# Scale rows gathered ahead, weights unpacked in the feed-forward, and the rotary sum on VectorE

## The reference

```python
q = _apply_rope(q, curr_seq_pos)
k = _apply_rope(k, curr_seq_pos)
raw = jnp.einsum('bhqd,bhkd->bhqk', q, k) / scale
attn = jax.nn.softmax(raw + mask, axis=-1)
...
w = (qw[:, None, :] >> shifts[None, :, None] & MAXQ).reshape(-1, qweight.shape[1])
s = scales[g_idx]
return (w.astype(scales.dtype) - z[g_idx].astype(scales.dtype)) * s
...
h = jax.nn.silu(xf @ Wg) * (xf @ Wu)
out = h @ Wd
```

## Time and profile before

| | |
|---|---|
| Median of 3 runs | 1169.86 us (1169.71 to 1169.95) |
| The profiled execution, its own time | 1171.48 us |
| Its span, first to last instruction | 1169.7 us |
| PE busy | 1037.1 us, 89% |
| DVE busy | 796.0 us, 68% |
| POOL busy | 457.7 us, 39% |
| ACT busy | 349.8 us, 30% |
| Mean granted TensorE clock | 0.946 of 2.4 GHz |

### The profile page before, as it was taken

How to read it: one execution, slowest core, us unless ns; L and a number is a source line. 1 busy time by engine, 2 the same in 40 slices (tenths; PEclk the granted TensorE clock), 3 DMA queues, 4 the chain that set the end, 5 groups by cost and what they waited for, 6 DMA issues and landing times. The chain is left out here.

```text
span 1169.7 us, 13349 instructions
## 1 busy us (share of the span) xinstructions
PE 1037.1 (89%) x4696; PEld 741.4 (63%) x4696; DVE 796.0 (68%) x1251; ACT 349.8 (30%) x926; POOL 457.7 (39%) x296
## 2 busy tenths in 40 slices
PE   5688877877878799999999999999999986999998
PEld 2333333344557567777777677677777765888787
DVE  4899998759566687778878888787676655222223
ACT  3232332213212332333333333333343332222131
POOL 3566655445515443444434434434243102222121
PEclk8899998869888899999999999999999998999999
DMA  7000000000311332332333325421010005211001
GB/s 258 1 1 0 1 1 1 1 18 1 104 50 52 118 123 78 127 112 88 109 100 118 126 80 168 161 97 45 27 46 18 1 2 168 53 38 32 1 1 72
DMA packets 60962, 75.91 MB, mean 65 GB/s; under 512 B 8444, under 2 KB 44068, under 8 KB 60888
## 3 DMA queue, kind: packets, MB, share of 16 engines
q1 hardware_dynamic: 56032, 57.66, 15.7%
q0 software_dynamic: 4144, 17.04, 4.5%
q10 hardware_dynamic: 720, 0.36, 0.1%
HBM read 64.37 MB, written 10.68 MB: 64 GB/s over the span
## 5 line engine op out<-in xcount | busy, mean ns | idle before, releaser
L1301 POOL TENSOR_TENSOR shared<-shared 128x512 f32<-128x512 f32 x64 | 83.7, 1307 | 201.6 <-DVE shared L1435 201.3
L754 PE MATMUL ps<-woh,oh 128*128 128x512 f32 x256 | 108.8, 425 | 32.9 <-DVE ol L1465 28.1
L1370 ACT ACTIVATE c_xn<-c_xn,c_mn 128x64 f32<-128x64 f32 x256 | 86.0, 337 | 155.6 <-DVE c_mn L1449 155.6
L754 PE MATMUL ps<-xh,wqh 128*128 128x512 f32 x256 | 106.6, 416 | 0.4 <-DVE shared L1435 0.4
L756 PE MATMUL ps<-woh,ol 128*128 128x512 f32 x256 | 104.7, 409 | 0.0
L755 PE MATMUL ps<-wol,oh 128*128 128x512 f32 x256 | 104.3, 408 | 0.0
L1433 DVE TENSOR_TENSOR shared<-ps,cs 128x512 f32<-128x512 f32 x80 | 54.9, 687 | 70.6 <-PE ps L756 70.6
L756 PE MATMUL ps<-xh,wql 128*128 128x512 f32 x256 | 100.4, 392 | 0.0
L755 PE MATMUL ps<-xl,wqh 128*128 128x512 f32 x256 | 99.9, 390 | 0.0
L540 DVE TENSOR_TENSOR r<-ps,vpad 128x512 f32<-128x512 f32 x128 | 79.4, 683 | 27.4 <-PE ps L629 27.4
L372 POOL TENSOR_TENSOR r<-r 128x1024 f32<-128x1024 f32 x32 | 77.1, 2410 | 50.4 <-DVE r L540 50.3
(11 more groups left out here) (172 smaller groups left out, 2387.8 us busy)
## 6 DMA issues: line engine op xcount, KB each, us to landing
stage<-in_wq SPq DMA_DIRECT2D x16, 512.0 KB, 4.1
stage<-in_wo SPq DMA_DIRECT2D x16, 512.0 KB, 3.8
w_wide<-dq SPq DMA_DIRECT2D x32, 172.0 KB, 4.9
wf<-w_wide SPq DMA_DIRECT2D x20, 256.0 KB, 3.4
qraw<-in_gate_qweight SPq DMA_DIRECT2D x16, 172.0 KB, 4.3
qraw<-in_up_qweight SPq DMA_DIRECT2D x16, 172.0 KB, 3.7
qraw<-in_down_qweight SPq DMA_DIRECT2D x10, 256.0 KB, 4.5
w_down<-dq SPq DMA_DIRECT2D x10, 256.0 KB, 6.0
```

The source lines that it names most:

```text
L754: pe.matmul(dst, lh, rh, start=(first and c == 0), stop=False)
L1301: pool.tensor_tensor(qT[:, h * TPH:(h + 1) * TPH, :, p - 1, :], turn(ra), turn(rb), ALU.add)\
L1370: act.activation(part, part, ACT.Exp, scale=-1.0, bias=mn[:, c % 2, u:u + 1], accum_out=sm[:, c % 2, u:u + 1]).then_inc(exp_ready, 1)
```

## The change

1. **Rotary sum.** `rotary_sum` is moved word for word from POOL's list to DVE's: behind `add` for the first rotary product of a step, right behind `rotary` for the second.
2. **Gate and up.** The attention steps no longer make these weights. POOL gathers their scale and zero rows, SP stores them as they are to a new HBM tensor `sz_wide`, and `gate_up` loads for each tile the packed integers (four loads of 64 KB, each row repeated eight times) and the rows of zeros and scales (two loads of 256 KB), and DVE unpacks, subtracts and multiplies there, into `wf`. Three buffers are used in turn.
3. **Down.** Its 11 units are made in the attention as before, but spread: `fetch_plan` gives every step number with n mod 4 = 2 a down unit and the others a gate/up unit, for n = 2 to 44. POOL issues the gather of step n's unit in step n-1, and waits first until the unit two before it in the plan is through (`fetch_done`): for a gate/up unit until its rows are stored, for a down unit until DVE has multiplied.
4. `wd` is loaded behind tile 5 instead of tile 3.

```diff
+def fetch_plan():
+    plan, wide, down, n = {}, 0, 0, 2
+    while wide < WIDE_UNITS or down < NTI:
+        if n % TPH == DOWN_AT and down < NTI:
+            plan[n] = (len(plan), WIDE_UNITS + down)
+            down += 1
+        elif n % TPH != DOWN_AT and wide < WIDE_UNITS:
+            plan[n] = (len(plan), wide)
+            wide += 1
+        n += 1
+    return plan
...
+def fetch_done(eng, g, f):
+    u = next(unit for number, unit in PLAN.values() if number == f)
     if u < WIDE_UNITS:
+        same = [v for number, v in PLAN.values() if number <= f and number % 2 == f % 2 and v < WIDE_UNITS]
+        eng.wait_ge(g["sz_stored"][f % 2], 16 * len(same))
     else:
+        eng.wait_ge(g["wd_ready"], u - WIDE_UNITS + 1)
...
+def fetch_scales(pool, g, f, u):
+    if f >= 2:
+        fetch_done(pool, g, f - 2)
+    table = g["table_wide"] if u < WIDE_UNITS else g["table_down"]
+    pool.indirect_dma_start(g["sz"][:, f % 2, 0:width_of(u)], None, table,
...
+def store_scales(sp, g, f, u):
+    chunk, q = u // QPIECES, u % QPIECES
+    sp.wait_ge(g["sz_landed"][f % 2], 16 * (f // 2 + 1))
+    sp.dma_start(g["sz_wide"][chunk * P:(chunk + 1) * P, :, q * QCOLS:(q + 1) * QCOLS],
...
 # rotary_attention, SP, step
                     load_number(PIECES * (2 * (b + db) + odd) + piece + 2)
-                u = unit_at(n)
-                if u is not None:
-                    if 2 <= u + 2 < Q_UNITS:
-                        load_packed(sp, a, g, u + 2)
-                    store_weights(sp, g, u)
+                if n - 1 in PLAN:
+                    f, u = PLAN[n - 1]
+                    if u < WIDE_UNITS:
+                        store_scales(sp, g, f, u)
+                    else:
+                        store_down(sp, g, u - WIDE_UNITS)
+                if n in PLAN and WIDE_UNITS <= PLAN[n][1] < Q_UNITS - 2:
+                    load_down(sp, a, g, PLAN[n][1] - WIDE_UNITS + 2)
...
 # rotary_attention, POOL, step
-                if projecting(c, last):
-                    for p in ROTARY_OF[j]:
-                        rotary_sum(b, sl + 1, p)
                 due = piece_due(c, last)
                 if due:
                     piece, db, odd = due
                     low_piece(pool, g, b + db, odd, piece)
-                u = unit_at(step_number(b, c))
-                if u is not None and u + 2 < Q_UNITS:
-                    gather_scales(pool, g, u + 2)
+                ahead = step_number(b, c) + 1
+                if ahead in PLAN:
+                    fetch_scales(pool, g, *PLAN[ahead])
...
 # rotary_attention, DVE, step
-                u = unit_at(step_number(b, c))
-                if u is not None:
-                    subtract_zeros(dve, g, u)
+                f, u = PLAN.get(step_number(b, c), (0, 0))
+                t = u - WIDE_UNITS
+                if t >= 0:
+                    subtract_zeros(dve, g, f, t)
                 units = ROTARY_OF[j] if projecting(c, last) else ()
                 for p in units[:1]:
                     rotary(b, sl + 1, p)
                 if tile_exists(c - 3, last):
                     add(b, c - 3, last)
+                for p in units[:1]:
+                    rotary_sum(b, sl + 1, p)
                 if early and tile_exists(c - 2, last):
                     low_out(b, c - 2)
                 if tile_exists(c, last):
                     probabilities(b, c)
-                if u is not None:
-                    multiply_scales(dve, g, u)
+                if t >= 0:
+                    multiply_scales(dve, g, f, t)
                 for p in units[1:]:
                     rotary(b, sl + 1, p)
-                if u is not None and u + 1 < Q_UNITS:
-                    unpack_weights(dve, g, u + 1)
+                    rotary_sum(b, sl + 1, p)
+                if 0 <= t < NTI - 1:
+                    unpack_down(dve, g, t + 1)
...
 # gate_up, SP
+                if k >= 3:
+                    sp.wait_ge(w_ready, k - 2)
+                for c in range(DC):
+                    src = bass.AP(q.tensor, q.offset + packed * c * INTER + P * t, [[INTER, packed], [0, PACK], [1, w]])
+                    sp.dma_start(raw[:, k % 3, c * P:c * P + w], src).then_inc(landed[k % 3], 16)
+                rows = g["sz_wide"][m * DC * P:(m + 1) * DC * P, :, t * P:t * P + w].rearrange("(c p) e n -> p e c n", p=P)
+                for e in range(2):
+                    sp.dma_start(columns(sz[:, k % 3, e, :], k), rows[:, e, :, :]).then_inc(landed[k % 3], 16)
+                if k == 5:
...
 # gate_up, DVE
+            for i in range(2, NT):
+                norm_rows(dve, g, n, xn, i)
+                norm_low(dve, g, n, XT, i - 2)
+                if i in DEQUANT_AT:
+                    dequantise(DEQUANT_AT[i])
+            norm_low(dve, g, n, XT, NT - 2)
+            norm_low(dve, g, n, XT, NT - 1)
+            dequantise(2)
+            dequantise(3)
             for t in range(NTI):
                 w = inner(t)
+                if t + 2 < NTI:
+                    unpack(2 * t + 4)
+                    subtract(2 * t + 4)
+                    unpack(2 * t + 5)
+                    scale(2 * t + 4)
+                    subtract(2 * t + 5)
+                    scale(2 * t + 5)
```

More of the change, by code:

```diff
@@ L853, in gather_scales @@
[L853 to L867, removed]
@@ L870, in subtract_zeros @@
[L870 to L886, removed]
@@ L889, in store_weights @@
[L889 to L899, removed]
+DOWN_AT = 2
+def fetch_plan():
[9 more added lines that the diff above has]
+    return plan
@@ new lines, in load_down, with unpack_down @@
+def load_down(sp, a, g, t):
+    rows = inner(t)
+    if t >= 2:
+        sp.wait_ge(g["q_used"], t - 1)
+    w = a["down_qweight"]
+    src = bass.AP(w.tensor, w.offset + P // PACK * t * D, [[D, rows // PACK], [0, PACK], [1, D]])
+    sp.dma_start(g["qraw"][0:rows, t % 2, :], src).then_inc(g["q_landed"][t % 2], 16)
+def unpack_down(dve, g, t):
+    raw = g["qraw"][0:inner(t), t % 2, :]
+    dve.wait_ge(g["q_landed"][t % 2], 16 * (t // 2 + 1))
+    dve.tensor_scalar(raw, raw, g["nib"][0:inner(t), 0:1], 15, ALU.logical_shift_right, ALU.bitwise_and).then_inc(g["qn_ready"], 1)
@@ new lines, in subtract_zeros, with multiply_scales @@
+def subtract_zeros(dve, g, f, t):
+    w = inner(t)
+    dve.wait_ge(g["qn_ready"], t + 1)
+    dve.wait_ge(g["sz_landed"][f % 2], 16 * (f // 2 + 1))
+    if t >= 2:
+        dve.wait_ge(g["w_stored"][t % 2], 16 * (t // 2))
+    dve.tensor_tensor(g["dq"][0:w, t % 2, :], g["qraw"][0:w, t % 2, :], g["sz"][0:w, f % 2, D:2 * D], ALU.subtract)\
+       .then_inc(g["q_used"], 1)
+def multiply_scales(dve, g, f, t):
+    w = g["dq"][0:inner(t), t % 2, :]
+    dve.wait_ge(g["q_used"], t + 1)
+    dve.tensor_tensor(w, w, g["sz"][0:inner(t), f % 2, 0:D], ALU.mult).then_inc(g["wd_ready"], 1)
@@ L903, in routed_lora, with store_down @@
+def store_down(sp, g, t):
+    rows = inner(t)
+    sp.wait_ge(g["wd_ready"], t + 1)
+    sp.dma_start(g["w_down"][t * P:t * P + rows, :], g["dq"][0:rows, t % 2, :]).then_inc(g["w_stored"][t % 2], 16)
 def routed_lora(nc, a, g):
@@ L1200, in rotary_attention @@
         g["dq"] = sb("dq", [P, 2, D])
-        for name in ("qn_ready", "q_used", "w_ready"):
+        for name in ("qn_ready", "q_used", "wd_ready"):
             g[name] = sem(name)
@@ L1510, in _ @@
                     rotary(0, 0, 0)
+                    rotary_sum(0, 0, 0)
             norm_low(dve, g, n, XT, NT - 2)
@@ L1676, in gate_up @@
         xn = sb("d_xn", [P, 2, D])
+        raw = sb("raw", [P, 3, D], I32)
+        sz = sb("d_sz", [P, 3, 2, D])
         wf = sb("wf", [P, 4, D])
@@ L1684, in gate_up @@
         step = sem("step")
-        wf_landed = [sem(f"wf_landed{i}") for i in range(4)]
+        landed = [sem(f"landed{i}") for i in range(3)]
+        qn_ready = sem("qn_ready")
+        q_used = sem("q_used")
+        w_ready = sem("w_ready")
         wd_landed = sem("wd_landed")
@@ L1740, in _ @@
                 norm_high(act, g, n, XT, i)
-                if i >= NT - 4:
-                    high(i - (NT - 4))
+                if i in DEQUANT_AT:
+                    high(DEQUANT_AT[i])
+            high(2)
+            high(3)
             for t in range(NTI):
```

103 lines of the change are left out of this document (56 added, 47 removed).

## The result

The change makes the kernel slower: 1204.5 us, median of 4 runs (1202.1 to 1206.2), against 1169.8 for the kernel before in the same comparison, a ratio of 1.0295 with a 95% interval of 1.0277 to 1.0313. That is +34.7 us where +45 was forecast, and inside the range. The profiled execution has a span of 1202.8 us (its own time 1204.6), so the two profiles differ by 33.1 us.

The account below looks back on a forecast made before the run. PE was taken as nearest to full, with dequantisation costing 34 us in the attention. Ten slots +38, first slot +1, tail +1 and gate/up +5 gave +45, so 1215 us, range 1170 to 1238.

Parts of the forecast that it names:

- The chain: Attention: POOL's low piece, SP's load and store, POOL's down gather, then DVE's subtraction; late rows stall PE 4.3 us a slot.
- ten slots: Attention steps 4 to 43 in fours, A to D, D without a projection: 43.0 us each forecast, +38 in all.
- The clock: PE's granted clock falls to 0.5 after the stall in each of the ten slots: 2.8 us lost a slot.
- The start: First slot of the attention: startup sums on DVE can be held up by wo low pieces, +1 us.
- The tail: Attention steps 44 to 59, no gathers for DVE: each `low_out` comes a sum later, +1 us in all.
- Gate/up: Start of the gate/up stage: more loads and dequantisation delay the first product, +5 us, ends +2 and +12.
- Rival 1: Scale rows land before 3.6 us in step C: stall 1.0 us, no clock loss, 1153 us; chance 0.15.
- rival 2: Scale rows late in step C but ahead of its low piece: stall 1.7, clock 1.7, 1177 us; chance 0.17.
- Rival 4: Sums still blocked between DVE and POOL, gathers hidden, nothing else: between -7 and +5 us; chance 0.03 for same time.
- The reading of the kernel before: Attention steps 4 to 43: PE's own slot is 35.8 us; dequantisation and its neighbours cost 3.4 a slot, 34 in all.

Follow-up runs that it names:

- e4: Changed kernel with the gate/up stage of the kernel before, leaving out dequantisation of the gate and up weights: 1194.3 us.
- e1: Changed kernel with SP's store of the scale rows put ahead of its load of the next weight piece: 1153.7 us.
- e9: Changed kernel with three buffers for the gathered scale rows instead of two, SP's order untouched: 1154.2 us.
- e10: As e9, with GpSimd's gather for the next step also put ahead of the step's low piece: 1152.7 us.
- e3: Kernel before with only the rotary sum moved to VectorE: 1150.0 us.
- e5: As e3, with VectorE's unpacking of a weight unit moved from the end of a step to just ahead of that unit's subtraction: 1138.7 us.
- e7: As e1, with ScalarE issuing scale-row loads of gate/up's first three tiles, and down weights loaded behind tile 7 instead of 5: 1155.7 us.

## Why the prediction was right

- **The chain**, the term that decided, held almost to the tenth, in all ten slots. Forecast for a slot with wo: store landed 13.0 us after the start of B, gather issued 0.3 later, rows there 17.6 after it; measured in the fifth slot: gather issued at 587.39 - 574.2 = 13.2, subtraction begun at 17.6 (12.8 to 13.4 and 17.3 to 17.6 in the five such slots). With wk, 12.6 and 16.9 were forecast, and the five slots have 12.3 to 12.6 and 16.7 to 16.9. `low_out` was to end 14.65 us after the start of C and ended at 14.6 in nine slots and 14.2 in the last; PE's stall was to be 4.3 and was 4.0.
- **The clock** was over-sized: 2.8 us a slot forecast, 2.1 measured. The row it came from had the clock low over 5.7 us after an idle of 3.8 us. Three slots lost as much (2.8 to 3.1 us); in the other seven it recovered sooner, in the fifth 2.9 us after the products began, although the idle was as long. Together with the stall that is 6.1 a slot for 7.2, 11 of the 11.4 us by which the ten slots were over-estimated (26.6 for 38).
- **The start** had the wrong sign: +1 forecast, -3.0 measured. That is outside the ends given for it, -0.7 and +2.8. The first scores came 0.9 us earlier (360.61 against 361.54), and the rest is gained in steps 0 to 3, which the forecast had left at nothing: ahead of the first output projection PE idles 4.93 us there instead of 6.08, and behind it the clock is low for 4.0 us instead of 6.0. **The tail** was 0 for +1.
- **Gate/up** was under-sized, 9.5 for 5, inside its ends: the first product came 6.7 us later and not 5.0 (SP needs 3.7 us a tile for six issues, not 3.0), and the loss of the clock behind the longer start (1.9) and the gap behind tile 6 (0.9) were not in the sum. e4 gets the whole of it back. The misses partly cancel: 11.4, 4 and 1 us too much for the slots, the start and the tail, and 4.5 too little here.
- **Rival 1** is what e1, e9 and e10 are: with the rows in time it forecast 1153, with a stall of 1.0 us and no loss of clock. They measured 1153.7, 1154.2 and 1152.7, with D at 6.0 instead of 5.1 in most slots and the clock at 0.99 to 1.00. Its deciding point, a landing 3.6 us into step C, was missed by 2.8 to 3.8 us in the changed kernel. But it is too strict: in e1 and e9 rows that come up to 5.2 us into C delay `low_out` by 0.3 us at most. What decides is C's low piece, at 6.1. Rival 2 needed rows ahead of that piece, and no slot had them, but in the five wk slots it was close: 6.4 to 6.7 us, as the forecast's 6.7 had it. Rival 4 is excluded by e3.
- **The reading of the kernel before** also held: dequantisation and its neighbours cost 34 us there, and e5 gets back 28.8 (363.4 for 392.2) without moving a unit to another stage. One thing in it was only true of some slots: the granted clock fell in four of the ten there, and of the four idles of 1.52 us it followed three. Those four slots lost 4.9 to 5.3 us and the other six 1.8 to 3.4, so rival 2's "stall 1.7 and clock 1.7" meets the mean of 3.4 without being what a slot there did.

From its issue to the gather that waited for it the store took 4.2 us (587.39 - 583.14), and the gather 4.4 until the subtraction began. The Trainium skill, DMA: Bandwidth & Descriptors, section on the anatomy of one DMA, would give 3.2 us for the gather by its figures, an estimate. The trace does not agree, and the landing times of the kernel before were the better basis. The forecast's 2.8 us for the store uses the same figures, but the section is on DMAs that GpSimd issues, and the store is SP's.

One thing stays open: why the clock came back sooner in seven slots than in the row that the forecast used, and not in three. The runs show the durations and not their cause.

## What to carry to other kernels

When work is moved away from a busy engine, follow what orders it as well as what it costs: here 35 us of VectorE's work went away, and one weight load ahead of one store cost 51 us, through SP, GpSimd, VectorE and PE. Two blocks changed about, or one buffer more, turned a loss of 35 us into a gain of 15 or 16; and the fastest version moves nothing between stages, only the sums to VectorE and one operation of 0.4 us out of the way of what PE waits for. The size of an engine's idle time alone says nothing of its price: ask which instruction stands behind each wait, and who needs it next.

## What the runs showed of the hardware

- A two-input operation of VectorE on SBUF is lengthened by what is left of a GpSimd tensor operation that it meets: the subtraction took 0.68 us in the clear, and 1.69, 2.39 and 2.94 us where it met a low piece (2.4 us), in the changed kernel, in e7 and in e1. In the two whose rows stand above it ended 0.55 us after the low piece (593.49 for 592.94, 647.55 for 647.00), as if it had begun only then; so it did in all ten slots of the changed kernel, whether the rows came 6.4 or 7.4 us into step C. That is what the Trainium skill, Trainium Architecture — The Big Picture, section on what this means for kernel authors, says of the port that the two engines share: "an exclusive lock (not a bandwidth split)"; the traces agree. So rows that come a little late can cost more than their lateness.
- The time of a gather scatters widely: in e1's profile the gathers of scale rows landed 3.9 to 7.6 us after their issue, median 5.7. The down gathers took 4.0 to 4.4 us in the changed kernel, where they left when the store had landed, 6.2 to 6.8 and once 7.6 in e1, where they left within 0.5 us of a weight load and a store, and 4.2 to 5.2 in e10. The two over 7.5 us, in e1 and e7 (8.1), made a slot over 5 us longer, the seventh both times.
- After idles of 3.7 to 4.1 us in the attention of the changed kernel, PE's lower clock level cost 1.6 to 1.8 us in seven slots and 2.8 to 3.1 in three; after an idle of 3.8 us in the kernel before it cost 2.8. Of four idles of 1.52 us there, three were followed by the lower level and one was not. The length of the one idle before it doesn't tell the loss.
